# Banded attention's last exponentials in free score banks, and the block attention's added bias laid down by TensorE

## The reference

```python
# banded attention: every token attends to itself and the 31 tokens before it
dot  = jnp.einsum('bthe,btkhe->bthk', q, kw)
attn = jax.nn.softmax(dot, axis=-1)
out  = jnp.einsum('bthk,btkhe->bthe', attn, vw)

# block attention: blocks of 32 queries, 32 keys and one block-mean key (33 keys)
scores = jnp.einsum('bnqhd,bnkhd->bnqkh', q, k) * scale
scores = scores + w_bias[None, :, :, :, None]          # the edge's weight
scores = jnp.where(mask[None, ..., None] == 0, -1e9, scores)
attn_probs = jax.nn.softmax(scores, axis=3)
out = jnp.einsum('bnqkh,bnkhd->bnqhd', attn_probs + gate, v)
```

## Time and profile before

| what | us |
|---|---|
| time, median of 3 runs | 602.98 (601.33 to 608.59) |
| span of the profiled execution | 606.4 |
| VectorE busy | 481.7 (79%) |
| TensorE matmuls busy | 419.3 (69%) |
| GpSimd busy | 340.5 (56%) |
| ScalarE busy | 196.1 (32%) |

### The profile page before, as it was taken

One profiled execution on the slowest core, in us unless ns is written; L12 is line 12 of the kernel. 1 busy time (PEld: TensorE's weight loads), 2 busy tenths in 40 slices (PEclk: granted clock), 3 DMA queues, 4 the chain that ended last, 5 costly groups with the idle time before them and its releaser, 6 DMA issues.

```text
span 606.4 us, 8743 instructions
## 1 busy us (share of the span) xinstructions
PE 419.3 (69%) x3283; PEld 206.2 (34%) x3283; DVE 481.7 (79%) x605; ACT 196.1 (32%) x221; POOL 340.5 (56%) x303
## 2 busy tenths in 40 slices
PE   6787854656677667666776898999283997454851
PEld 2452323222232223222222344577252436331320
DVE  1999998899999999999999336989936569984242
ACT  2665793323323322323322062410021045112210
POOL 6767103659999998999999431699960000520000
PEclk8977987769999999999999989955575995567567
DMA  8640023935554556445451000000000000000000
GB/s 286 182 141 9 3 79 80 211 94 142 148 155 146 149 147 165 140 139 175 143 152 51 0 13 2 1 2 2 2 24 0 1 0 2 1 2 9 3 5 35
DMA packets 29523, 46.11 MB, mean 76 GB/s; under 512 B 18146, under 2 KB 19588, under 8 KB 28452
## 3 DMA queue, kind: packets, MB, share of 16 engines
q1 hardware_dynamic: 27044, 45.12, 26.2%
q0 software_dynamic: 2368, 0.37, 0.5%
q10 hardware_dynamic: 64, 0.00, 0.0%
HBM read 43.57 MB, written 1.11 MB: 74 GB/s over the span
## 4 chain that ended last, share of the span: by engine, by line
DVE 33%; POOL 29%; PE 19%; issue 13%; ACT 3%; DMA 2%; DVEq 1%; ACTq 0%; POOLq 0%; SPq 0%
POOL dBu L888 14%; POOL hit L872 6%; PE ps L2035 4%; POOL work L965 3%; DVE hC L1546 3%; PE ps L2363 2%; DVE hC L1316 2%; POOL work L970 2%; DVE hst L1525 2%; POOL work L954 2%; DVE hC L1312 2%; PE ps L2542 2%; PE ps L2532 1%; DVE work L1798 1%; PE ps L2243 1%
## 5 line engine op out<-in xcount | busy, mean ns | idle before, releaser
L2173 PE MATMUL ps<-hC,ident 128*128 128x512 f32 x256 | 122.4, 600 | 0.0
L1163 ACT ACTIVATE ps<-work,a_neg 128x1020 f32<-128x1020 f32 x64 | 71.2, 1115 | 153.9 <-DVE hst L1525 102.7
L1525 DVE TENSOR_TENSOR_SCAN hst<-ps,dBu 128x1024 f32<-128x1024 f32 x43 | 98.3, 2286 | 5.1 <-POOL dBu L888 3.8
L2157 PE MATMUL ps<-late,pick_state 96*128 96x512 bf16 x128 | 40.4, 398 | 70.4 <-DVE hC L1546 68.3
L872 POOL DMA_INDIRECT hit<-in_L_attn_edge_values,tab_i x64 | 64.8, 1012 | 29.5 <-DMA hit<-in_L_attn_edge_values,tab_i 20.1
L888 POOL TENSOR_TENSOR dBu<-work,dA 128x1024 f32<-128x1024 f32 x32 | 75.4, 2360 | 6.7 <-DMA dA<-b_rows_all 4.0
L2173 PEld LDWEIGHTS ps<-hC,ident 128*128 128x128 f32 x256 | 49.6, 194 | 43.3 <-issue 34.9
L888 POOL TENSOR_TENSOR dBu<-work,b_sb 128x1024 f32<-128x1024 f32 x16 | 39.6, 2475 | 38.7 <-DVE dA L1454 37.2
L1546 DVE TENSOR_TENSOR hC<-hst,ps 128x1024 f32<-128x1024 f32 x43 | 51.5, 1197 | 1.8 <-PE ps L2157 1.0
L1525 DVE TENSOR_TENSOR_SCAN work<-ps,dBu 128x1024 f32<-128x1024 f32 x21 | 48.0, 2286 | 2.6 <-POOL dBu L888 1.8
L2157 PEld LDWEIGHTS ps<-late,pick_state 96*128 96x128 bf16 x128 | 7.9, 98 | 121.8 <-DVE hC L1546 116.4
(11 more groups left out here) (374 smaller groups left out, 821.9 us busy)
## 6 DMA issues: line engine op xcount, KB each, us to landing
dA<-b_rows_all SPq DMA_DIRECT2D x64, 256.0 KB
b_sb<-b_rows_all SPq DMA_DIRECT2D x32, 256.0 KB
work<-b_rows_all SPq DMA_DIRECT2D x32, 256.0 KB
work<-in_L_attn_edge_index SPq DMA_DIRECT2D x6, 1024.0 KB, 6.5
dA<-in_L_attn_edge_index SPq DMA_DIRECT2D x1, 1024.0 KB, 5.0
dBu<-in_L_attn_edge_index SPq DMA_DIRECT2D x1, 1024.0 KB, 8.3
hit<-in_L_attn_edge_values,tab_i POOLq DMA_INDIRECT x64
late<-work SPq DMA_DIRECT2D x12, 64.0 KB, 2.0
```

The costliest lines, as they stand in the source:

```text
L1163: nc.scalar.activation(dst[:, :, 1:], src[:, :, 1:], ACT.Exp, scale=a_neg[:, n:n + 1]).then_inc(dA_sb, 1)
L1525: V.tensor_tensor_scan(h_buf[i % 3], dA_ps[k], dBu[:, k, :], 0.0, ALU.mult, ALU.add).then_inc(scan_done, 1)
L2157: last = T.matmul(bank(2 + h), pick_state[:, n, :, :].rearrange("p v i -> p (v i)"), parts[:, j * NT + h * HALF:j * NT + (h + 1) * HALF], ...
L2173: last = T.matmul(bank(6 + h), ident[:, :], hC[:, i % 2, h * HALF:(h + 1) * HALF], start=False, stop=(n == S - 1))
```

## The change

The last unit's exponentials are written to PSUM banks 0 and 1 instead of back into the SBUF buffer; the sums and the scaling of that unit read them there. In the block attention TensorE first writes `added` into each of the four banks by a matmul with the identity and lets the score products accumulate on it; VectorE's L1794 and its semaphore are gone, maximum and subtraction read the banks, and the banks are free for the next image only at `s3_shift`.

```diff
+        last_exp = bank(0, 2)
-        s3_read = sem("s3_read")
@@ ScalarE
-                nc.scalar.activation(s2_buf[u % 3], s2_buf[u % 3], ACT.Exp).then_inc(s2_exp, 1)
+                nc.scalar.activation(last_exp if u == UNITS - 1 else s2_buf[u % 3], s2_buf[u % 3],
+                                     ACT.Exp).then_inc(s2_exp, 1)
@@ VectorE, window_sums
-                link(V.tensor_reduce(sm2[:, u % 2, :], s2_buf[u % 3].rearrange("p (s k) -> p s k", k=C),
-                                     AX_X, ALU.add))
+                src = last_exp if u == UNITS - 1 else s2_buf[u % 3]
+                link(V.tensor_reduce(sm2[:, u % 2, :], src.rearrange("p (s k) -> p s k", k=C), AX_X, ALU.add))
@@ VectorE, last_windows
-                link(V.tensor_tensor(seg, seg, sm2[:, u % 2, :].unsqueeze(2).to_broadcast([P, SEGS, C]), ALU.mult))
+                link(V.tensor_tensor(seg, last_exp.rearrange("p (s k) -> p s k", k=C),
+                                     sm2[:, u % 2, :].unsqueeze(2).to_broadcast([P, SEGS, C]), ALU.mult))
@@ VectorE, block_scores
-                keys = s3[j].rearrange("p (s k) -> p s k", k=KN)
+                by_block = lambda t: t.rearrange("p (g b) -> p g b", g=G)
+                keys = ps[:, 0:4, 0:BL * KN].rearrange("p g (b k) -> p g b k", k=KN)
                 dve.wait_ge(s3_ps, j + 1)
-                V.tensor_tensor(s3[j].rearrange("p (g x) -> p g x", g=G), ps[:, 0:4, 0:BL * KN],
-                                added.unsqueeze(1).to_broadcast([P, G, BL * KN]), ALU.add).then_inc(s3_read, 1)
-                dve.wait_ge(s3_read, j + 1)
-                link(V.tensor_reduce(mx3[:, j, :], keys, AX_X, ALU.max))
-                V.tensor_tensor(keys, keys, mx3[:, j, :].unsqueeze(2).to_broadcast([P, G * BL, KN]),
+                link(V.tensor_reduce(by_block(mx3[:, j, :]), keys, AX_X, ALU.max))
+                V.tensor_tensor(s3[j].rearrange("p (g b k) -> p g b k", g=G, k=KN), keys,
+                                by_block(mx3[:, j, :]).unsqueeze(3).to_broadcast([P, G, BL, KN]),
                                 ALU.subtract).then_inc(s3_shift, 1)
@@ TensorE, block_scores
+                for g in range(G):
+                    T.matmul(bank(g)[:, 0:BL * KN], ident[:, :], added, start=True, stop=False,
+                             skip_group_check=True)
                 for b in range(BL):
                     for g in range(G):
                         r = slice(C * g, C * g + C)
                         last = T.matmul(bank(g)[:, b * KN:(b + 1) * KN],
                                         q3[r, j * BL + b, :, :].rearrange("p h q -> p (h q)"),
-                                        k3[r, j * BL + b, :], start=True, stop=True)
+                                        k3[r, j * BL + b, :], start=False, stop=True, skip_group_check=True)
@@ TensorE, between the images
-                pe.wait_ge(s3_read, j)
+                pe.wait_ge(s3_shift, j)
```

## The result

The changed kernel takes 608.88 us (603.45 to 615.46, 20 runs) against 604.38 us (600.88 to 608.91, 20 runs) for the kernel before on the same chip. The ratio is **1.0052, with a 95% interval of 1.0028 to 1.0077**: 3 us slower, 1.7 to 4.7 with the interval. By medians it is 4.5 us. The ratio leaves out three long runs of the changed kernel, those of 612.67 us and more, which its median takes in. The direction is clear of the noise, the size is about half a per cent.

The account below looks back on a forecast made before the run. GpSimd's hold on VectorE was taken to bound the banded attention's end, VectorE the block attention. Saving 2.4 us and losing 7.3 gave +4.9 on a 602.98 median: 607.9 us, range 602 to 613.

Parts of the forecast that it names:

- Part A: End of banded attention: last exponentials in PSUM free VectorE's scaling from GpSimd's hold, saving 2.4 us.
- The rival that gave part A nothing: Banded attention: freed VectorE is held at the band product by GpSimd's gathers too; total +7.3 us, chance 0.1.
- The series: Block attention: bias matmuls, scores, maximum and subtraction run serially, 9.94 us an image at clock 0.50, 6.52 at 1.00.
- part B: Block attention: TensorE lays down the bias instead of VectorE adding it, costing 7.3 us.
- The tail: Block attention, last subtraction to the residual L1861: VectorE's work in the same order, kept at 9.30 us.
- The clock: TensorE's clock in block attention: rises in some images, two of four score groups at 1.00, saving 3.3 us.
- The clock high in all images: Rival, block attention: identity matmuls keep TensorE's clock up for all four images; total -5.5, 597.5 us, chance 0.1.
- The clock low throughout: Rival, block attention: TensorE's clock stays at 0.50 for the whole stage; total +8.2, 611.2 us, chance 0.25.

Follow-up runs that it names:

- e1: Kernel before with only the last unit's exponentials moved to PSUM, block attention unchanged: ratio 0.9930, median 600.58 us.
- e5: Kernel before with one edit, TensorE's next scores wait for the subtraction instead of the first read: ratio 1.0019, block-attention stage 31.4 us.
- e7: Whole change with its full 128-row bias matmuls, images 1 and 3 in banks 4 to 7, no wait for the subtraction: ratio 0.9953, stage 25.5 us.
- e6: Whole change plus six matmuls of zeros in TensorE's idle time after the scores of images 1 and 2: ratio 0.9990, stage 28.2 us.
- e3: Whole change with the bias laid down by four 32-row matmuls, one per row group: ratio 0.9925, stage 28.4 us.
- e4: Whole change with the bias in 32-row groups and images 1 and 3 in banks 4 to 7: ratio 0.9898, stage 25.9 us.
- e2: Kernel before with only the bias by TensorE, banded attention unchanged: ratio 1.0111, median 610.57 us.

## Why the prediction was right, point by point

**Part A** held step by step. I gave L1674 1.23 us, it took 1.18. The transpose did wait for GpSimd's product; the band product behind it (L1664 before, L1665 after) was held by GpSimd's last product and ended 0.95 us behind it (I took 1.08). From GpSimd's first product of unit 5 to TensorE's output I had 437.4 - 429.53 = 7.9 us; it was 7.75. The saving, 2.4 forecast, is 2.5 in the profiles of the change and of e1. The rival that gave part A nothing fell with e1: the gathers behind the products did not hold VectorE.

**The series** of part B held. At 0.50 I worked out 9.94 us an image, measured 10.12; at 1.00 6.52, measured 6.64. The small excess is in the bias matmuls: 3.81 us from the first of them to the first score matmul where I had 3.57, and 1.98 where I had 1.79. The row I took the price from, L2035's 3.46 us, was no pure row at 0.50: as I say myself further down, the clock rose within it. e5 has the wait without the bias matmuls (31.4 us), e7 the bias matmuls without the wait (25.5 us, at 1.00): in neither does the stage grow by the 6.1 us of the change.

**The tail** from the last subtraction to the residual, which I kept at 9.30 us, is 9.27 (533.86 to 543.13).

**The clock** was the open term, and it was the right one to leave open: the clock rose near the end of a bias group, and two images stayed at 0.50. That it would be two of the four score groups was a guess, which no row decided, and it came out by luck and in another way than I told it: I expected the clock to rise in some images and to be low again for the next. It rose once, in image 0, was still up for image 1, and the bias matmuls of images 2 and 3, 3.89 us each, did not raise it again. So what was mis-sized is what a rise is worth. I counted two score groups at 1.00, 3.3 us. It was image 0's scores and all of image 1, bias matmuls too: (10.12 - 8.32) + (10.12 - 6.64) = 5.3 us. With the bias matmuls' excess the other way, part B cost 6.1 instead of 7.3 us, and the sum is +3.5 by profile against my +4.9.

**The rivals.** The clock high in all images needed TensorE to stay at work: e6 and e7 bring that about from image 0's scores on, with stages of 28.2 and 25.5 us. e6 is serial like the change, and my price holds there: 26.0 us for four images at 1.00, and 1.8 more for image 0's bias matmuls, which were still at 0.50, make 27.8. So the rival's 3.1 us would have been only about 1. In the change itself the idle time that I had named against it brought the clock down. The clock low throughout would have made four images of 10.1.

**The total.** Forecast 607.9 on a median of 602.98; measured 608.88 on 604.38. The median of three runs that I forecast on was 1.4 us low against twenty, and part B's forecast was 1.2 us over what the profile shows, so part of the closeness is luck; the difference, +4.9 forecast against +3.1 by the ratio and +4.5 by medians, is the fairer measure.

## What to carry to other kernels

Moving work to an idle engine moves its waits too: before an accumulator is filled by a second pass, ask when its bank comes free, and whether the engine that used to run ahead now takes turns with the one that it was meant to relieve. In the profiled stage a second set of banks was worth at least as much here as laying the bias down in 32-row groups (25.5 us in e7, 28.4 in e3); by the totals the two cannot be told apart. Where an instruction on VectorE with two SBUF operands lasts several times its usual time beside GpSimd, an operand in PSUM can free it, as it did here (6.41 to 1.18 us), and the next such instruction in line can inherit the hold. Price TensorE at both clocks, and look at what stands in its idle time.

## What the runs showed of the hardware that I had not expected

**A hold can outlast one instruction.** VectorE's L1674 before was held through three GpSimd products that followed one another without a gap, 5.3 us; the same kind of hold after the change, met by one product, cost 0.8 us (1.89 against 1.09). Both ended about 1 us after GpSimd's last product (1.08 and 0.95), so here the length of GpSimd's unbroken run set the hold.

**TensorE at work without a gap stayed at the low clock.** e4's TensorE worked from 507.30 to 520.40 without a pause, on groups of 32 rows, and the clock was at 0.50 all the time. e7's did the same scores with 128-row bias matmuls among them and was at 1.00 from 502.30 to 522.80, pauses included. A bias group did not always raise it: image 0's ended with the clock up in the change, e2, e6 and e7, those of images 2 and 3 left it at 0.50 in the change and in e2. Why is open.

**The untouched stretches moved by 2 us.** From the residual to the end, windows of before and of after:

```profile
541.00:606.00 65.00, 34.75 (x356) 14.31 (x356) 24.67 (x49) 11.05 (x14) 0.00 (x0) 0.66 0.05 13
```

```profile
543.00:606.00 63.00, 31.78 (x356) 12.61 (x356) 24.98 (x50) 11.06 (x14) 0.00 (x0) 0.74 0.05 13
```

The same 356 TensorE records took 34.75 us in the one execution and 31.78 in the other, at a mean clock of 0.66 and 0.74. The stretch itself differs by 2.3 us, about what part A is worth. Two spans that agree to 0.1 us say little here; the stretches, cut at the same instructions, say which part did what.
